# FFN norms: the first value of the inverse root from a logarithm and an exponential of ScalarE, in place of ScalarE's square root and VectorE's reciprocal

## The reference

```python
q = (hidden_states @ Wq + bq).reshape(B, S, H, QD)          # 8 heads of 64
q = (q - mean) / jnp.sqrt(var + EPS_BN) * bn_gamma + bn_beta
q0 = _l2norm(q[..., :HALF])                                  # x / max(norm, 1e-12)
q1 = _l2norm(q[..., HALF:])
s0 = jnp.einsum('bshq,kq->bshk', q0, k0)                     # 32 keys per half
s1 = jnp.einsum('bshq,kq->bshk', q1, k1)
ts0, ti0 = jax.lax.top_k(s0, 4); ts1, ti1 = jax.lax.top_k(s1, 4)
# 16 sums of pairs, softmax over them, w picks among 32 * 32 experts (only 256 exist)
eh = gelu(down[idx] . hidden); out = sum of up[idx] * eh * w
```

## Time and profile before

| | us |
|---|---|
| median of 3 runs | 405.86 |
| lowest and highest | 405.62 and 405.95 |
| span of the profiled execution, first to last instruction | 403.8 |
| what lies around the span (median less span) | 2.1 |
| FFN norms begin (first L1807 in the span) | 309.85 |

### The profile page before, as it was taken

How to read it: one execution, slowest core, us unless ns; L and a number is a source line. 1 busy time by engine, 2 the same in 40 slices (tenths; PEclk the granted TensorE clock), 3 DMA queues, 4 the chain that set the end, 5 groups by cost and what they waited for, 6 DMA issues and landing times.

```text
span 403.8 us, 7801 instructions
## 1 busy us (share of the span) xinstructions
PE 395.0 (98%) x2584; PEld 367.1 (91%) x2584; DVE 300.1 (74%) x1093; ACT 237.8 (59%) x519; POOL 215.9 (53%) x209
## 2 busy tenths in 40 slices
PE   8999999999999999999999999999999999999877
PEld 7878888899999999999999999999788899999766
DVE  5797768786757867476864848572986989899996
ACT  3886859454764466464545434342557977779462
POOL 1788999764385333153430300000166858989993
PEclk9999999999999999999999999999999969999999
DMA  7900213004434312233211000000100000000102
GB/s 226 310 2 1 83 55 102 8 11 128 128 89 121 118 30 59 58 84 104 65 47 30 2 0 2 1 2 2 27 1 2 0 2 2 28 28 27 41 28 67
DMA packets 19992, 21.38 MB, mean 53 GB/s; under 512 B 3180, under 2 KB 16624, under 8 KB 19952
## 3 DMA queue, kind: packets, MB, share of 16 engines
q1 hardware_dynamic: 18832, 19.96, 16.5%
q10 hardware_dynamic: 1120, 0.92, 0.7%
HBM read 18.78 MB, written 2.10 MB: 52 GB/s over the span
## 4 chain that ended last, share of the span: by engine, by line
PE 80%; POOL 12%; DVE 4%; issue 3%; DMA 1%; ACT 0%; SPq 0%; DVEq 0%; POOLq 0%; ACTq 0%
PE keep_pQ L75 11%; PE keep_pQ L76 11%; PE keep_pQ L77 11%; POOL ffn_prod L1258 9%; PE context_pA L1051 6%; PE context_pA L1053 6%; PE context_pA L1052 6%; PE context_pR L1085 6%; PE context_pR L533 3%; PE context_pA L533 3%; POOL ffn_near L1326 2%; PE ffn_pK L1807 2%; PE context_pR L75 2%; PE context_pR L77 2%; PE context_pR L76 2%
## 5 line engine op out<-in xcount | busy, mean ns | idle before, releaser
L899 DVE TENSOR_TENSOR att_pTl<-context_pR,att_pTh 128x512 fp32r<-128x512 f32 x64 | 36.9, 586 | 29.8 <-ACT att_pTh L811 29.5
L811 ACT ACTIVATE att_pTh<-context_pR 128x512 fp32r<-128x512 f32 x64 | 32.1, 514 | 40.1 <-PE context_pR L1085 40.1
L1258 POOL TENSOR_TENSOR ffn_prod<-ffn_first,ffn_near 128x1024 f32<-128x1024 f32 (+1 forms) x29 | 54.1, 1885 | 2.1 <-DVE ffn_first L1684 2.1
L851 ACT ACTIVATE att_prob<-keep_pQ,att_nmax 128x1206 f32<-128x1206 f32 x16 | 20.3, 1269 | 35.9 <-DVE att_nmax L935 35.8
L930 DVE TENSOR_REDUCE att_mx<-keep_pQ 128x1 f32<-128x402 f32 x64 | 34.5, 564 | 6.9 <-PE keep_pQ L77 6.6
L1837 PE MATMUL ffn_pT<-keep_ident,ffn_prod 128*128 128x128 f32 x240 | 30.5, 283 | 3.7 <-POOL ffn_prod L1258 3.7
L1837 PEld LDWEIGHTS ffn_pT<-keep_ident,ffn_prod 128*128 128x128 f32 x240 | 28.6, 148 | 5.8 <-DVE ffn_hT L1717 4.8
L786 POOL TENSOR_TENSOR keep_rstd<-att_ve,keep_mhalf 128x4 f32<-128x4 f32 x3 | 3.0, 1007 | 55.9 <-DVE att_ve L989 55.9
L1085 PE MATMUL context_pR<-keep_ident,att_prob 128*128 128x128 f32 (+1 forms) x208 | 31.8, 272 | 0.2 <-DVE att_pTl L899 0.2
L1051 PE MATMUL context_pA<-att_pTh,att_cNh 128*128 128x256 f32 (+1 forms) x104 | 31.0, 298 | 0.0
L1051 PE MATMUL context_pA<-att_pTh,context_cNh 128*128 128x256 f32 (+1 forms) x104 | 30.9, 297 | 0.0
(11 more groups left out here) (336 smaller groups left out, 1300.3 us busy)
## 6 DMA issues: line engine op xcount, KB each, us to landing
keep_raw<-in_ctxT SPq DMA_DIRECT2D x24, 256.0 KB, 2.7
keep_raw<-in_ctx SPq DMA_DIRECT2D x24, 256.0 KB, 3.0
out<-keep_x SPq DMA_DIRECT2D x16, 128.0 KB, 1.7
keep_x<-in_x SPq DMA_DIRECT2D x3, 512.0 KB, 9.9
gru_wout<-in_W_out SPq DMA_DIRECT2D x1, 512.0 KB, 8.7
keep_raw<-in_fWq SPq DMA_DIRECT2D x2, 256.0 KB
keep_raw<-in_ctxT SPq DMA_DIRECT2D x8, 32.5 KB, 3.1
keep_raw<-in_ctx SPq DMA_DIRECT2D x4, 65.0 KB
```

Of the source, the lines that this page charges most:

```text
L811: act.activation(to, bank, ACT.Copy).then_inc(bank_high, 1)
L899: dve.tensor_tensor(to, bank, half(it, 0, n)[0].bitcast(F32), ALU.subtract).then_inc(bank_free, 1)
L1258: return eng.tensor_tensor(prod[:, i % PB, a:b].rearrange("p h (i j) -> p h i j", j=KEYS), (factor if factor is not None else first[:, n % ...
```

## The change

`nroot` becomes `nlog`, and ACT takes two steps, a logarithm and the exponential of minus half of it, both from one table set that is loaded ahead of the first batch and again after the late Gelus. DVE's reciprocal goes. `ny`, which DVE wrote to PSUM, is now written by ACT to an SBUF tile; the three operations of the Newton step read it there.

```diff
+LOG_EXP = "natural_log_exp_and_others"
...
-    n2, nroot, nt, nu = (st.sb(n, [P, MOST]) for n in ("n2", "nroot", "nt", "nu"))
+    n2, nlog, ny, nt, nu = (st.sb(n, [P, MOST]) for n in ("n2", "nlog", "ny", "nt", "nu"))
...
-    ny = pB[:, 128:128 + MOST]
...
         def norm_roots(k):
             act.wait_ge(n2_ready, k + 1)
             m = len(BATCHES[k]) * PER * HALVES
-            act.activation(nroot[:, 0:m], n2[:, 0:m], ACT.Sqrt).then_inc(nroot_ready, 1)
+            act.activation(nlog[:, 0:m], n2[:, 0:m], ACT.Ln).then_inc(nlog_ready, 1)
+            act.wait_ge(nlog_ready, k + 1)
+            act.activation(ny[:, 0:m], nlog[:, 0:m], ACT.Exp, scale=-0.5).then_inc(nroot_ready, 1)
...
         squared(0)
         gelu(EARLY_GELU - 1)
+        act.preload_act_table_set(LOG_EXP)
         norm_roots(0)
...
                 for m in range(EARLY_GELU, ES):
                     late_gelu(m)
+                act.preload_act_table_set(LOG_EXP)
...
             dve.wait_ge(nroot_ready, k + 1)
-            a = note(dve.reciprocal(yy, nroot[:, 0:m]))
-            yield
-            need(a)
             a = note(dve.scalar_tensor_tensor(out=t, in0=n2[:, 0:m], scalar=-0.5, in1=yy, op0=ALU.mult,
                                               op1=ALU.mult))
```

More of the change, by code:

```diff
@@ L1201, in stage_ffn @@
     mv_ready, avg_mm, bn_ready = st.sem("mv_ready"), st.sem("avg_mm"), st.sem("bn_ready")
-    sq_ready, sq_pool, norm_mm, n2_ready, nroot_ready, ninv_ready = (
-        st.sem(n) for n in ("sq_ready", "sq_pool", "norm_mm", "n2_ready", "nroot_ready", "ninv_ready"))
+    sq_ready, sq_pool, norm_mm, n2_ready, nlog_ready, nroot_ready, ninv_ready = (
+        st.sem(n) for n in ("sq_ready", "sq_pool", "norm_mm", "n2_ready", "nlog_ready", "nroot_ready", "ninv_ready"))
     q_ready_dve, q_ready_pool, q_ready_act = (st.sem(n) for n in ("q_ready_dve", "q_ready_pool", "q_ready_act"))
```

## The result

The changed kernel takes 414.13 us in the median (413.91 to 414.37, 4 runs), against 405.9 us for the kernel before on the same chip. The ratio is 1.0213, with a 95% interval of 1.0193 to 1.0232. That is 8.2 us slower; forecast were 6.7, and 412.6 us in a range of 408.2 to 416.0. The span of the profiled execution is 412.2 us, 8.4 more. The 405.9 rests on four runs; the 23 runs of the kernel before that were made beside experiments 1, 2, 3 and 8 have a median of 405.09, and against that the loss is 9.0 us.

The account below looks back on a forecast made before the run. The path was taken to run from batch 2's norms through DVE to POOL's selections and products, then PE. Terms 2.4 + 1.4 + 2.5 + 0.4 = 6.7 us on 405.86 gave 412.6 us, range 408.2 to 416.0.

Parts of the forecast that it names:

- part 4: `ny` in SBUF: each Newton operation on DVE, now with two SBUF inputs, waits for a POOL operation under way.
- Parts 1 to 3: Fewer ACT table loads, logarithm and exponential for the root, no DVE reciprocal: alone a gain of 0.3 to 1.1 us.
- the loads don't matter: ACT's table loads around the roots lie in its idle time; dropping 10.3 us of them costed at nothing on the path.
- Batches 0 and 1: Three DVE waits each for POOL pieces, 1.2 then 0.5 us; 1.06 taken up by DVE's idle time, leaving +0.6.
- Batch 2: Newton operations wait for a POOL selection and product; the selection of 334.59 comes 1.8 + 0.6 = 2.4 us later.
- Batch 3: Newton operations wait for POOL's second and third products; `remove(6)` moves from 349.3 to 353.1, 1.4 us new.
- the clock's fall: Rival, chance 0.07: longer holes in PE ahead of the norms of group 6 bring half clock, +3.5 us, thus 416.
- Batch 4: L1622 waits for POOL's products to end at 374.2; `remove(10)` moves from 368.40 to 374.7, 2.5 us new.
- The pushes: Behind each DVE operation that gets in, POOL's next starts about 0.13 us later; three count, +0.4 us.
- The signs to look for: Profile after: Newton operations at 1 us or more, POOL idle 2 us ahead of tiles 6 and 10, four FFN table loads.

Follow-up runs that it names:

- experiment 1: The changed kernel with the exponential's result `ny` in PSUM, where the reciprocal's was, in place of SBUF; ratio 0.9972 to the kernel before, median 403.79 us.
- Experiment 2: The kernel before, square root and reciprocal kept, with only the reciprocal's result moved from PSUM to an SBUF tile; ratio 1.0234, median 414.61 us.
- experiment 3: The changed kernel with `ny` still in SBUF, but the other Newton tiles `n2`, `nt` and `nu` in PSUM; ratio 0.9978, median 404.11 us.
- experiment 8: The changed kernel with twelve useless matmuls filling TensorE's hole ahead of the norms of group 6; ratio 1.0174, median 412.08 us.
- experiment 5: The changed kernel with `ny` in SBUF for batch 2 alone and in PSUM for the other batches; ratio 1.0042 to the kernel before.
- experiment 12: The kernel of experiment 1 with the last expert product moved behind the norms of batch 2's first group; ratio 0.9974, median 404.38 us.

## Why the prediction was right

- **The mechanism held.** The step on which all hung, part 4, was that an operation with two SBUF inputs waits for the POOL operation under way, even at 128x32 or 128x64 elements. Experiment 2 shows that the placement alone makes the loss, 1.0234. Experiments 1 and 3 show that either input in PSUM takes it away. VectorE and GpSimd thus meet here without a semaphore, which the description of the core at the start of the document leaves out.
- **Parts 1 to 3 held in sum.** They were priced at 0.3 to 1.1 us of gain if alone. Experiment 1 has 0.28% of 405, 1.1 us (0.4 to 1.9), the upper end. Which part brings how much is not shown, and the profiles don't show the 1.1: that of experiment 1 and that of before, both at half clock from 326, differ by 0.2 us from the start of the norms to tile 11. That the loads don't matter held for those in front of the logarithm only; the preload is what keeps one from coming behind it.
- **Batches 0 and 1** were put at waits of 1.2 and 0.5 us, of which 0.6 would stay. In the changed kernel the three operations took 1.2 and 0.7 us longer than in the kernel before. Alone these batches cost 0.6, with an interval that reaches to nothing.
- **Batch 2** was put at 1.8. In the changed kernel batches 0 to 2 made 1.7 us of shift in place of 2.4, and batch 2 alone cost 2.8. In the profile of before TensorE ran at half clock around 327; in the changed kernel's it did not, so it gave back part of the loss at that place. Against experiment 3's profile, at full clock as well, the shift is 2.8. The prediction let a delay at 334.59 pass whole to the end. It was read from a profile with half clock at 326, and in such a profile only 0.2 of batch 2's 1.8 us were left at tile 11 (experiment 5).
- **Batch 3** was put at 1.4 and made 1.5 at tile 6. Then 2.0 us followed ahead of tile 9 that the sum didn't have. This is the term that was missing: I had it as a rival of its own, the clock's fall, with 0.07 and 3.5 us, and against it the rows where holes of 1.6 and 1.7 us had kept the full clock. Experiment 8 shows it: 2.0 us with the hole filled. The forecast and this rival came together, and the rival was underrated, though its 3.5 us were too much.
- **Batch 4** was put at 2.5. It made 2.3 + 0.4 in the changed kernel, and 2.9 alone, where 2.5 to 2.8 was expected.
- **The pushes** of 0.4 us for POOL: no run shows this term. The prediction gives no row for its 0.13 us; that is how far behind a Newton operation DVE's next instruction starts, not POOL's. Three products took 5.66 and 5.70 us where it had been 5.65 and 5.66.
- **The total was in part luck.** In the span, 2.0 us of clock and 0.6 us that stood there before the norms began were not in the sum, and 0.7 at batches 0 to 2 and 0.4 of pushes were too much. The profile of before had the half clock at 326 and the changed kernel's had not, which made the difference between them smaller by some 2.5 us. Counted from the start of the norms the changed kernel's tile 11 is 7.9 us later than in the profile of before, and 10.5 later than in experiment 3's. Experiments 1 and 3, worth the same by their ratios, are themselves 2.5 us apart there, with the half clock and without it.
- **The signs to look for.** POOL idle by 2.2 us ahead of tiles 6 and 10, DVE busier with less to do, four table loads, ACT down by 8.7: all there. That each of the three operations would have a mean of 1 us or more was too simple. In each batch of 128x64 the operations that meet POOL at work are slow, up to 1.84 us, and the one that meets it idle takes 0.2.

The version to keep is that of experiment 1, 0.9972 (0.9953 to 0.9991). It is faster than both kernels and computes the same steps as the changed one.

## What to carry to other kernels

When a small tile moves from PSUM to SBUF, look at who reads it. In every batch of this kernel a VectorE operation whose inputs were then both in SBUF waited for GpSimd's operation of the moment, and a chain of such operations could wait once for each link. Price it by the length of GpSimd's operations, not by that of the small one, and look for the proof in the kernel's own trace, where some tiny operation takes a microsecond now and 0.15 at other times. A wait that opens a hole in TensorE's work can cost a second time by its clock. And before you price a delay from one profile, see whether TensorE's clock fell in it: batch 2's waits left 0.2 us at tile 11 in a profile with a fall ahead of them, and cost 2.8 us in the average of the runs.

## What the runs showed of the hardware beyond that

- **The granted clock differs between runs of one kernel.** In the 23 runs of the kernel before beside experiments 1, 2, 3 and 8, a mean clock of 1.0 went with spans of 402.2 to 403.0 us (8 runs) and one of 0.992 with 403.8 to 404.7 (6 runs); the other nine, at 0.995 or 0.996, lie between and across, 402.4 to 404.2. For experiment 1 it was 401.2 to 401.8 and 403.7. The two levels show in windows of two profiles, experiment 1 and experiment 3, same work on TensorE:

```profile
326.00:333.00 7.00, 7.00 (x35) 7.00 (x35) 4.59 (x40) 2.48 (x9) 2.90 (x3) 0.51 0.00 1
```

```profile
326.00:333.00 7.00, 7.00 (x55) 6.64 (x55) 5.54 (x50) 3.23 (x11) 3.05 (x3) 1.00 0.00 1
```

  Around the fall TensorE ran 16 matmuls of 4 columns, 8 of 128 and again 16 of 4, in experiment 1's profile with the fall and in experiment 3's without it, so the order alone doesn't bring it. With an expert product moved between (experiment 12) none of 12 runs had a mean clock of 0.992, against 3 of 12 in experiment 1; six had 0.995 or 0.996, at spans of 402.8 to 403.3. Whether the order has a part in it is open. The mean is a coarse sign, too: experiment 12's profile has a mean of 1.0, and half clock from 401 to 403.8.
- **The same hole brought the fall in one run and not in another.** TensorE is idle for 2.91 us ahead of its sums at 385.18 in the changed kernel, and for 2.91 us ahead of the same sums at 382.86 in experiment 8. From 383 to 387 the granted clock is 1.00 in the first and 0.57 in the second.
- **A fall cost nothing where GpSimd set the pace.** Experiment 8's profile is at half clock from 339 to 343 too. POOL's selections of tiles 3 and 6 stand 17.8 us apart in it, as in the changed kernel, which is at full clock there. At 359, where DVE waited for TensorE's sums, the fall cost 2.0 us.
- **A pair of functions that share a set need not be served by it.** Logarithm and exponential got two loads a batch until the set was named by a preload.
